# One product with padded weights of 128 columns for the scan inputs of both directions of an orientation

## The chip, the cores and the metric

The kernel runs on one core of one Trainium2 chip. The metric is the device time of one execution in microseconds (us). Everything is float32. The engines of a core are TensorE (PE in the profile, its weight loads PEld), VectorE (DVE), ScalarE (ACT), GpSimd (POOL) and SyncE (SP), which issues the transfers here.

## The reference, cut to what matters

A batch of 8 images of 384 channels and 32 x 32 positions goes through four layers, each with a residual: attention with 12 heads and a depthwise 5 x 5 convolution (layer 0), a selective scan over four directions (layer 1), a blur with fixed shifts (layer 2), attention and a gate (layer 3). The change is in the scan:

```
xs = [x by rows, x by columns, x by rows reversed, x by columns reversed]   # 4 directions, 384 x 1024 each
x_dbl = einsum('bkdl,kcd->bkcl', xs, x_proj_weight)                         # 44 values per position and direction
dts, Bs, Cs = x_dbl[:, :, :12], x_dbl[:, :, 12:28], x_dbl[:, :, 28:]
dt = softplus(einsum('bkrl,kdr->bkdl', dts, dt_projs_weight) + bias)
h = h * exp(dt * A) + (dt * u) * Bs;   y = sum over the 16 states of h * Cs
```

The two directions of one orientation (rows, or columns) read the same positions, one forwards and one backwards; only the 44 columns of weights differ.

## The kernel before

**Stages.** An image's scan has 192 steps: four sets (one for each direction, in the order columns, columns reversed, rows, rows reversed; `DIRS`), each with 3 chunks of 128 channels and 16 states. Set k covers steps 48 k to 48 k + 47. While image i is scanned, the same engines do layer 0 of image i + 1 (`early`, three head groups with four heads each) and layers 2 and 3 of image i - 1 (`late`). The first image's layer 0 runs alone ahead of it, the last image's layers 2 and 3 alone behind it. A loop (`Fori`) covers images 1 to 6; the first and last are written out.

**Order.** Each engine runs one list of events in order of a due time that is counted in scan steps (`scan_events`, `late_events`, `early_events`, sorted by `in_order`). No engine overtakes in its list; semaphores join the lists.

**A scan step**: ScalarE makes the decay (event a, line 1239), VectorE the drive (b, line 1660) and the scan (s, line 1670), GpSimd multiplies the state by its row of C (h, line 1353), and three steps later TensorE adds the transposed state into PSUM banks 4 and 5 (z, line 980). Rows of B and C come from HBM, spread over all partitions, through SyncE (lines 601 and 609).

**Inputs of a set.** Event x, one for each half of 512 positions, is three products of 128 x 44 weights (line 953), which the profile shows as six matmul instructions, into 44 rows of bank 0, and a ScalarE copy to `xdbl` (line 1209), at partitions 0 to 43 for an even set and 64 to 107 for an odd one. The second half waits for the copy of the first. Event W stores the 32 rows of B and C of the set (line 589), K loads the weights for dt (line 593), and d (line 963) multiplies the last 12 rows into dt, through bank 0 again. The x-events of set k are due at 48 k - 21.3 and 48 k - 20.3, those of the next image's set 0 at step 180.7 and 181.7. So set 1 falls beside the blur of the image before, set 2 into the scores of the first head group and set 3 into the middle head group.

**A head group** has a part with scores for the row maxima (S, line 863, read by line 1590) and a part of 32 events T. A T makes transposed scores in banks 0 and 1 (line 883), ScalarE takes their exponentials (line 1180), and the next T waits for that. V (line 892) multiplies by the values into bank 2, Z (line 897) sums into bank 3. After 16 T's the first half of the queries is done: VectorE takes the reciprocal of bank 3 (line 1597) and multiplies it by bank 2 (line 1599). The V that opens the second half waits for line 1599. Between these, VectorE adds terms of the depthwise convolution (line 1609). The same pair of lines closes the second half. This document calls the passage between the two halves the turn.

The lines that say what a T and a V wait for:

```
                    if scans and a:
                        pe.wait_ge(t_exp.h, t_exp.at(img, a))
...
                    if kb == 0 and qh == 1:
                        pe.wait_ge(o_sb.h, o_sb.at(img, 2 * g + 1))
```

**The blur** stores its result to HBM (line 635) and loads it again by channels (line 638); line 1705 adds it. **The start**: line 575 loads the constants, then VectorE prepares small tables and zeroes some tiles (lines 1475 to 1754) and takes the statistics of the first image (line 1502).

Of the kernel before, what the change touches and what calls it, by code (L numbers as in the profile page):

```python
# [6 lines left out]
ACT = mybir.ActivationFunctionType  # L7
# [5 lines left out]
P = 128  # L13
NC = C // P
LB = L // P
HALF = 512
# [8 lines left out]
K, R, N = 4, 12, 16  # L25
XR = R + 2 * N
# [40 lines left out]
def scan_events(first, last):  # L67
# [19 lines left out]
    for run in range(STEPS1 // GN_):  # L87
        u = GN_ * run + GN_ + LAG
# [6 lines left out]
    for k in range(1, K + 1):  # L95
        ahead = -22 if k < K else -12
        if k == K and last:
            continue
        for hf in range(2):
            out.append((PER * k + ahead + hf + 0.70, ("x", k // K, k % K, hf)))  # L100
        out.append((PER * k + ahead + 2.5, ("W", k // K, k % K)))
        out.append((PER * k + ahead + 4.0, ("K", k // K, k % K)))
# [8 lines left out]
    for i in range(STEPS1 + SLOTS):  # L111
        for kind, late in (("B", 1.0), ("C", 2.3)):
            at = i - SLOTS + late
# [186 lines left out]
def build(nc, t):  # L300
    ctx = ExitStack()
    with ctx:
        def sb(name, cols, parts=P):
            return ctx.enter_context(nc.sbuf_tensor(name, [parts, cols], F32))
# [3 lines left out]
        def sem(name, per, first=1):  # L308

            s = Signal(ctx.enter_context(nc.semaphore(name)), per, first)  # L310
            if per:
                signals.append(s)
            return s
# [7 lines left out]
        negA = sb("negA", K * NC * N)  # L321
        w_xproj = sb("w_xproj", NC * K * XR)
        w_dt = sb("w_dt", C)
# [165 lines left out]
        xc_in = sem("x1_loaded", 16 * NC)  # L489
        xd_ps = sem("xproj_in_psum", 2 * K)  # L490
        xd_sb = sem("xproj_evacuated", 2 * K)
        bc_st = sem("bc_rows_stored", 16 * K)
# [75 lines left out]
        def _(sp):  # L568
            for s in signals:
                sp.sem_inc(s.h, s.first)  # L570
            for name, dst in [("ident", ident[:, :]), ("group_avg", group_avg[:, :]), ("vecs", vecs[:, :]),
                              ("vec96", vec96[0:QC3, :]), ("lepe_w", lepe_w[:, :]), ("A_logs", negA[:, :]),
                              ("w_xproj", w_xproj[:, :]),
                              ("row_index", R_[:, 0:1]), ("col_row", R_[:, 32:64])]:
                sp.dma_start(dst, t[name]).then_inc(c_in.h, 16)
# [9 lines left out]
            def scan(img, kind, k, first=False):  # L585
                if kind == "W":
                    at = 64 * (k % 2)
                    sp.wait_ge(xd_sb.h, xd_sb.at(img, 2 * k + 2))
                    sp.dma_start(bc_d[k], xdbl[at:at + 2 * N, :]).then_inc(bc_st.h, 16)
# [147 lines left out]
        def _(pe):  # L737
# [188 lines left out]

            wx = w_xproj[:, :].rearrange("p (c k r) -> p c k r", c=NC, k=K)

            def scan(img, kind, k, u=0, first=False):
# [13 lines left out]
                if kind == "x":  # L943
                    if k == 0 and u == 0:
                        pe.wait_ge(gu_out.h, gu_out.at(img, 1))
                    if u:
                        pe.wait_ge(xd_sb.h, xd_sb.at(img, 2 * k + 1))
                    elif k or not first:
                        pe.wait_ge(dt_abs.h, dt_abs.at(img, 2 * NC * k))
                    for c in range(NC):  # L950
                        rhs = U[:, c, :]
                        rhs = transposed(rhs)[:, u * 16:u * 16 + 16, :] if cols else rhs[:, u * HALF:(u + 1) * HALF]
                        mm = pe.matmul(ps[0:XR, 0, :], wx[:, c, cols + 2 * back, :], rhs, start=c == 0, stop=c == NC - 1)  # L953
                    mm.then_inc(xd_ps.h, 1)
                if kind == "d":
                    c, hf = u // 2, u % 2
                    at = 64 * (k % 2) + 32
                    if u == 0:
                        pe.wait_ge(xd_sb.h, xd_sb.at(img, 2 * k + 2))
                        pe.wait_ge(wd_in.h, wd_in.at(img, 16 * (k + 1)))  # L960
                    else:
                        pe.wait_ge(dt_abs.h, dt_abs.at(img, 2 * NC * k + u))
                    pe.matmul(ps[:, 0, :], w_dt[at:at + R, c * P:(c + 1) * P], xdbl[at:at + R, hf * HALF:(hf + 1) * HALF],  # L963
                              start=True, stop=True).then_inc(dt_ps.h, 1)
# [171 lines left out]
        def _(act):  # L1136
# [60 lines left out]
            def scan(img, kind, k, u=0, first=False):  # L1197
# [4 lines left out]
                if kind == "x":  # L1202
                    act.wait_ge(xd_ps.h, xd_ps.at(img, 2 * k + u + 1))
                    at = 64 * (k % 2)
                    if u == 0 and k >= 2:
                        act.wait_ge(bc_st.h, bc_st.at(img, 16 * (k - 1)))
                    elif u == 0 and not first:
                        act.wait_ge(bc_st.h, bc_st.at(img - 1, 16 * (K + k - 1)))
                    act.activation(xdbl[at:at + XR, u * HALF:(u + 1) * HALF], ps[0:XR, 0, :], ACT.Copy).then_inc(xd_sb.h, 1)
                if kind == "d":  # L1210
# [196 lines left out]
        def _(v):  # L1407
# [163 lines left out]
            def u_free(img):  # L1571

                v.wait_ge(dt_sb.h, dt_sb.at(img, K * NC))
                v.wait_ge(xd_sb.h, xd_sb.at(img, 2 * K))

# [96 lines left out]
            def late(img, kind, u=0, alone=False):  # L1672
# [70 lines left out]
                if kind == "fx":  # L1743
                    m = u
                    if m == 0:
# [3 lines left out]
                                           ALU.mult, ALU.add).then_inc(f_sb.h, 1)  # L1749

            v.memset(negm[:, :], 0.0)
            v.memset(k2[1], 0.0)
# [91 lines left out]
```

## Time and profile before

| | |
|---|---|
| median of 3 runs | 10391.47 us (10388.24 to 10403.53) |
| the profiled execution | 10405.13 us, its span 10403.3 us |
| VectorE busy | 8089.8 us, 78% |
| TensorE busy | 7344.5 us, 71%, mean granted clock 0.786 |
| GpSimd busy | 4789.0 us, 46% |
| ScalarE busy | 4060.0 us, 39% |
| products of line 953 | 384 instructions, 289.2 us busy |

A busy share is a mean over stages with different limits: none of the engines is busy throughout. An image takes some 1,260 us. In the rows, a line of the timeline gives the start, the duration, the engine, the line of the kernel, the operation, what it writes and reads, how many instructions are merged in it, and in brackets how long the engine was idle before it and what ended that. The granted clock is TensorE's as a share of 2.4 GHz, so 0.50 is 1.2 GHz.

### The profile page before, as it was taken

The page shows a single profiled execution, that of the slowest core. Times are in us where ns is not written, and L with a number is a line of the kernel's source. Part 1 is how long each engine was busy: PE and PEld are TensorE (multiplying, and loading weights), DVE is VectorE, ACT ScalarE, POOL GpSimd, SP SyncE. Part 2 cuts the span into 40 slices and gives each one's busy share as a digit, 9 for nine tenths or more (in the row PEclk, how much of TensorE's full clock was granted, in tenths as well). Part 3 has the DMA queues.
Part 4 walks back from the last instruction along what each step waited for, and adds up shares of the span by engine and source line. Part 5 has one row for each costly group of instructions (what it writes and reads, how often), then busy time and mean ns, then how long its engine had stood idle before and what let it go on. Part 6 is the DMA issues. An engine that isn't in the chain of part 4 may idle for free.

```text
span 10403.3 us, 101295 instructions
## 1 busy us (share of the span) xinstructions
PE 7344.5 (71%) x33720; PEld 3729.0 (36%) x33720; DVE 8089.8 (78%) x5527; ACT 4060.0 (39%) x4186; POOL 4789.0 (46%) x1990
## 2 busy tenths in 40 slices
PE   6757775777758777586776777677775777757556
PEld 2233334433334333342234432343333433244333
DVE  5477888778885888768987688876888678887992
ACT  3333443344433444334443345433443334433431
POOL 2154554345553454435644355434555345543660
PEclk8857877888769878688887878787886888868657
DMA  0174457544574445744566445664447544575782
GB/s 26 42 234 160 164 184 235 197 144 165 187 250 164 159 165 201 237 159 160 174 216 220 158 163 170 234 198 162 164 163 246 196 154 160 189 232 198 253 272 58
DMA packets 717961, 1875.97 MB, mean 180 GB/s; under 512 B 258896, under 2 KB 274640, under 8 KB 717264
## 3 DMA queue, kind: packets, MB, share of 16 engines
q1 hardware_dynamic: 717392, 1869.00, 54.0%
q8 instruction: 281, 4.60, 0.2%
q14 instruction: 288, 2.36, 0.1%
HBM read 1772.03 MB, written 71.04 MB: 177 GB/s over the span
## 4 chain that ended last, share of the span: by engine, by line
PE 40%; DVE 32%; issue 14%; ACT 7%; DMA 4%; DVEq 2%; SPq 1%; ACTq 1%; POOL 0%; POOLq 0%
DVE R L1670 14%; PE ps L751 8%; DVE ps L1660 8%; PE ps L883 7%; PE ps L980 5%; ACT R L1180 4%; DVE nmx L1590 4%; PE ps L1068 3%; PE ps L892 3%; PE ps L863 2%; PE ps L953 2%; PE ps L1051 2%; PE ps L963 1%; PE ps L845 1%; PE ps L1037 1%
## 5 line engine op out<-in xcount | busy, mean ns | idle before, releaser
L1353 POOL TENSOR_TENSOR R<-R 128x1024 f32<-128x1024 f32 x1536 | 3673.5, 2392 | 4302.2 <-DVE ps L1660 4198.6
L1670 DVE TENSOR_TENSOR_SCAN R<-R,ps 128x1024 f32<-128x1024 f32 x1536 | 3508.0, 2284 | 176.3 <-ACT R L1239 62.7
L1239 ACT ACTIVATE R<-R,negA 128x1024 f32<-128x1024 f32 x1536 | 1749.4, 1143 | 2313.4 <-DVE R L1670 2273.6
L980 PE MATMUL ps<-ident,R 128*128 128x128 f32 x12288 | 2146.9, 335 | 587.6 <-POOL R L1353 545.9
L980 PEld LDWEIGHTS ps<-ident,R 128*128 128x128 f32 x12288 | 1806.3, 175 | 1576.1 <-issue 775.2
L1660 DVE TENSOR_TENSOR ps<-R 128x1024 f32<-128x1024 f32 x1536 | 2030.5, 1322 | 162.1 <-DMA R<-bc_scratch 53.7
L1180 ACT ACTIVATE R<-ps 128x1024 f32<-128x1024 f32 x768 | 785.6, 1023 | 1061.8 <-PE ps L883 1061.8
L863 PE MATMUL ps<-R 32*128 32x512 f32 x3072 | 660.1, 943 | 678.8 <-DVE nmx L1590 585.7
L883 PE MATMUL ps<-R 64*128 64x512 f32 x3072 | 900.9, 665 | 203.2 <-ACT R L1180 108.0
L1590 DVE TENSOR_REDUCE nmx<-ps 128x4 f32<-128x2048 f32 x384 | 873.4, 2282 | 193.8 <-PE ps L863 190.6
L751 PE MATMUL ps<-R 128*128 128x512 f32 (+1 forms) x1824 | 879.2, 640 | 201.9 <-DVE R L1525 142.2
L1360 POOL TENSOR_TENSOR R<-R 128x1024 f32<-128x1024 f32 x312 | 824.3, 2642 | 331.2 <-ACT R L1173 269.5
L751 PEld LDWEIGHTS ps<-R 128*128 128x128 f32 (+1 forms) x1824 | 356.7, 200 | 664.5 <-issue 600.7
L1609 DVE SCALAR_TENSOR_TENSOR R<-R,lepe_w 128x1024 f32<-128x1024 f32 x264 | 514.7, 1950 | 26.0 <-issue 3.4
L1173 ACT ACTIVATE R<-R,lepe_w 128x1024 f32<-128x1024 f32 x312 | 361.0, 1159 | 346.6 <-POOL R L1360 346.0
L863 PEld LDWEIGHTS ps<-R 32*128 32x128 f32 x3072 | 167.7, 257 | 894.5 <-DVE nmx L1590 742.9
L892 PE MATMUL ps<-R 128*32 128x512 f32 x3072 | 432.0, 636 | 54.5 <-DVE R L1599 51.4
L883 PEld LDWEIGHTS ps<-R 64*128 64x128 f32 x3072 | 240.6, 191 | 636.2 <-ACT R L1180 419.6
L1345 POOL TENSOR_TENSOR R<-R 128x1024 f32<-128x1024 f32 x96 | 253.1, 2637 | 437.4 <-DVE R L1651 437.4
L1597 DVE RECIPROCAL R<-ps 128x512 f32<-128x512 f32 x48 | 161.1, 3357 | 335.1 <-PE ps L897 335.1
L897 PE MATMUL ps<-R,ones 128*32 128x512 f32 x3072 | 411.0, 607 | 0.0
L761 PE MATMUL ps<-ident,R 128*128 128x128 f32 x1280 | 220.6, 331 | 227.4 <-DVE R L1689 68.0
(157 smaller groups left out, 5615.0 us busy)
## 6 DMA issues: line engine op xcount, KB each, us to landing
R<-bc_scratch SPq DMA_DIRECT2D x3072, 512.0 KB, 4.5
R<-in_x SPq DMA_DIRECT2D x72, 512.0 KB, 7.1
out<-R SPq DMA_DIRECT2D x72, 512.0 KB, 5.3
R<-shift_scratch SPq DMA_DIRECT2D x48, 640.0 KB, 7.4
R<-R SPq DMA_DIRECT2D x192, 128.0 KB
R<-out SPq DMA_DIRECT2D x48, 512.0 KB, 8.4
R<-in_w_qkvo SPq DMA_DIRECT2D x32, 576.0 KB, 8.3
rows_scratch<-R SPq DMA_DIRECT2D x24, 512.0 KB, 7.4
```

The lines of the kernel that those rows point to most:

```text
L751: mm = pe.matmul(dst[0:parts, hf * HALF:(hf + 1) * HALF], lhs[:, c], rhs(c, hf), start=c == 0, stop=c == NC - 1)
L863: mm = pe.matmul(ps[:, bank + r, :], q4[HD * r:HD * r + HD, g, qc * P:(qc + 1) * P], k4[HD * r:HD * r + HD, g, hf * HALF:(hf + 1) * HALF], ...
L883: mm = pe.matmul(ps[:, bank + j, :], k2[pair][rows, kb * P:(kb + 1) * P], q2[g][pair][rows, qh * HALF:(qh + 1) * HALF], start=True, stop=True)
L892: pe.matmul(ps[HD * r:HD * r + HD, 2, :], vT[:, kb, P * g + HD * r:P * g + HD * r + HD], pT[(2 * a + r // 2) % 4][:, r % 2, :], start=kb = ...
L980: mm = pe.matmul(ps[:, 4 + b // 4, (b % 4) * P:(b % 4 + 1) * P], state[i % HELD][:, b * P:(b + 1) * P], ident[:, :], start=fresh and i % G ...
L1180: act.activation(pT[a % 4].rearrange("p j q -> p (j q)"), banks(bank), ACT.Exp).then_inc(t_exp.h, 1)
L1239: act.activation(decay[i % len(decay)], dt[:, c, :], ACT.Exp, scale=negA[:, col:col + 1]).then_inc(a_sb.h, 1)
L1353: pool.tensor_tensor(state[i % HELD], state[i % HELD], rows_c[slot], ALU.mult).then_inc(hc_sb.h, 1)
L1360: pool.tensor_tensor(heads[:, m, :], heads[:, m, :], tapped[n % 2], ALU.add).then_inc(dw_sb.h, 1)
L1590: v.tensor_reduce(nmx4[:, :, qc, hf], ps[:, bank:bank + 4, :], AX.X, ALU.max, negate=True)\
L1660: v.tensor_tensor(drive, dtu[:, c, :], rows_b[slot], ALU.mult).then_inc(b_sb.h, 1)
L1670: v.tensor_tensor_scan(h, a, b, 0.0, ALU.mult, ALU.add).then_inc(h_sb.h, 1)
```

## The change

The weights of the two directions of one orientation stand side by side in one tile of 128 columns for each chunk: 44 columns of one, 20 of zeros, 44 of the other, 20 of zeros. One x-event then gives the inputs of two sets: its product fills all 128 partitions of bank 0, and one ScalarE copy brings them to `xdbl`, where the odd set's rows land at partition 64 as before. So x-events are left only for sets 0 and 2; those of sets 1 and 3 are gone, and the events W and d of the odd sets wait for the copy of the even one. The copy for set 2 overwrites all of `xdbl` and so waits for the stores of both sets before it. `w_xproj` is loaded to a free part of the large tile `R` at the start, and VectorE zeroes the padded tile and copies the weights into it, six copies of 2 x 44 columns.

```
-        for hf in range(2):
+        for hf in range(2 * (k % 2 == 0)):
             out.append((PER * k + ahead + hf + 0.70, ("x", k // K, k % K, hf)))
...
-        w_xproj = sb("w_xproj", NC * K * XR)
+        w_xproj = sb("w_xproj", NC * 2 * P)
...
-        xd_ps = sem("xproj_in_psum", 2 * K)
-        xd_sb = sem("xproj_evacuated", 2 * K)
+        xd_ps = sem("xproj_in_psum", K)
+        xd_sb = sem("xproj_evacuated", K)
...
-                              ("w_xproj", w_xproj[:, :]),
+                              ("w_xproj", R_[:, 256:256 + NC * K * XR]),
...
                 if kind == "W":
                     at = 64 * (k % 2)
-                    sp.wait_ge(xd_sb.h, xd_sb.at(img, 2 * k + 2))
+                    sp.wait_ge(xd_sb.h, xd_sb.at(img, k // 2 * 2 + 2))
...
-            wx = w_xproj[:, :].rearrange("p (c k r) -> p c k r", c=NC, k=K)
+            wx = w_xproj[:, :].rearrange("p (c o m) -> p c o m", c=NC, o=2)
...
                     if u:
-                        pe.wait_ge(xd_sb.h, xd_sb.at(img, 2 * k + 1))
+                        pe.wait_ge(xd_sb.h, xd_sb.at(img, k + 1))
...
-                        mm = pe.matmul(ps[0:XR, 0, :], wx[:, c, cols + 2 * back, :], rhs, start=c == 0, stop=c == NC - 1)
+                        mm = pe.matmul(ps[:, 0, :], wx[:, c, cols, :], rhs, start=c == 0, stop=c == NC - 1)
...
                     if u == 0:
-                        pe.wait_ge(xd_sb.h, xd_sb.at(img, 2 * k + 2))
+                        pe.wait_ge(xd_sb.h, xd_sb.at(img, k // 2 * 2 + 2))
...
-                    act.wait_ge(xd_ps.h, xd_ps.at(img, 2 * k + u + 1))
-                    at = 64 * (k % 2)
-                    if u == 0 and k >= 2:
-                        act.wait_ge(bc_st.h, bc_st.at(img, 16 * (k - 1)))
+                    act.wait_ge(xd_ps.h, xd_ps.at(img, k + u + 1))
+                    if u == 0 and k:
+                        act.wait_ge(bc_st.h, bc_st.at(img, 16 * k))
                     elif u == 0 and not first:
-                        act.wait_ge(bc_st.h, bc_st.at(img - 1, 16 * (K + k - 1)))
-                    act.activation(xdbl[at:at + XR, u * HALF:(u + 1) * HALF], ps[0:XR, 0, :], ACT.Copy).then_inc(xd_sb.h, 1)
+                        act.wait_ge(bc_st.h, bc_st.at(img - 1, 16 * K))
+                    act.activation(xdbl[:, u * HALF:(u + 1) * HALF], ps[:, 0, :], ACT.Copy).then_inc(xd_sb.h, 1)
...
+            v.memset(w_xproj[:, :], 0.0)
+            v.drain()
+            raw = R_[:, 256:256 + NC * K * XR].rearrange("p (c b o r) -> p c b o r", c=NC, b=2, o=2)
+            padded = w_xproj[:, :].rearrange("p (c o b r) -> p c o b r", c=NC, o=2, b=2)
+            for c in range(NC):
+                for o in range(2):
+                    v.tensor_copy(padded[:, c, o, :, 0:XR], raw[:, c, :, o, :])
             v.memset(negm[:, :], 0.0)
```

## Rows read from the trace of the kernel before

**Rows 1.** Chain that ended last, 3770 to 3790 us: its shares by line.
```profile
by line: PE ps L883 27.9%; PE ps L953 27.8%; ACT R L1180 20.7%; PE ps L980 10.2%; PE ps L892 9.9%; ACT R L1209 3.0%; issue 1.8%; ACTq L1179 0.2%
```

**Rows 2.** Timeline, middle head group's turn, image 2 (start us, duration us, ...).
```profile
3771.85 1.06 PE L892 MATMUL ps<-R 128*32 128x512 f32 x8
...
3775.83 1.09 PE L980 MATMUL ps<-ident,R 128*128 128x128 f32 x8
...
3777.91 1.06 PE L897 MATMUL ps<-R,ones 128*32 128x512 f32 x8
...
3779.04 3.36 DVE L1597 RECIPROCAL R<-ps 128x512 f32<-128x512 f32 x1 [10.24 <-PE ps L897]
3779.10 2.77 PE L953 MATMUL ps<-R,w_xproj 128*44 128x512 f32 x6
...
3782.55 1.13 PE L883 MATMUL ps<-R 64*128 64x512 f32 x4 [0.68 <-ACT R L1209]
...
3783.61 1.07 PE L892 MATMUL ps<-R 128*32 128x512 f32 x8
...
3784.61 1.09 PE L980 MATMUL ps<-ident,R 128*128 128x128 f32 x8
...
3786.69 1.07 PE L897 MATMUL ps<-R,ones 128*32 128x512 f32 x8
```

**Rows 3.** Timeline, third head group's turn, image 2.
```profile
3992.57 3.36 DVE L1597 RECIPROCAL R<-ps 128x512 f32<-128x512 f32 x1 [7.23 <-PE ps L897]
...
3996.74 1.94 PE L892 MATMUL ps<-R 128*32 128x512 f32 x8 [2.99 <-DVE R L1599]
...
4001.35 1.07 PE L897 MATMUL ps<-R,ones 128*32 128x512 f32 x8
```

**Rows 4.** Timeline, third head group's turn, image 3.
```profile
5250.13 3.36 DVE L1597 RECIPROCAL R<-ps 128x512 f32<-128x512 f32 x1 [7.23 <-PE ps L897]
...
5254.31 1.07 PE L892 MATMUL ps<-R 128*32 128x512 f32 x8 [2.99 <-DVE R L1599]
...
5257.39 1.06 PE L897 MATMUL ps<-R,ones 128*32 128x512 f32 x8
```

**Rows 5.** Timeline, first head group's turn, image 2.
```profile
3559.93 3.36 DVE L1597 RECIPROCAL R<-ps 128x512 f32<-128x512 f32 x1 [5.20 <-PE ps L897]
...
3564.11 1.93 PE L892 MATMUL ps<-R 128*32 128x512 f32 x8 [2.99 <-DVE R L1599]
...
3569.88 1.07 PE L897 MATMUL ps<-R,ones 128*32 128x512 f32 x8
```

**Rows 6.** Windows: us, PE, PEld, DVE, ACT, POOL busy, PEclk, DMA share, GB/s.
```profile
3997.00:4000.00 3.00, 3.00 (x15) 1.39 (x8) 2.91 (x3) 0.00 (x0) 0.00 (x0) 0.50 0.00 0
...
5252.00:5255.00 3.00, 0.69 (x8) 0.16 (x8) 2.83 (x4) 1.50 (x2) 0.00 (x0) 1.00 0.00 0
```

**Rows 7.** Timeline, middle head group's end, image 2.
```profile
3821.89 1.07 PE L897 MATMUL ps<-R,ones 128*32 128x512 f32 x8
...
3823.74 3.35 DVE L1597 RECIPROCAL R<-ps 128x512 f32<-128x512 f32 x1
```

**Rows 8.** Timeline, inputs of set 1 and the blur's end, image 2.
```profile
3070.19 5.36 PE L953 MATMUL ps<-R,w_xproj 128*44 128x512 f32 x6
...
3081.57 3.36 DVE L1705 TENSOR_TENSOR R<-R 128x3072 f32<-128x3072 f32 x1 [4.08 <-DMA R<-blur_scratch]
```

**Rows 9.** Weight loads by line and form: count, busy us, mean ns, idle before.
```profile
L751 PEld LDWEIGHTS ps<-R 128*128 128x128 f32 x1440 | 289.6, 206 | 517.2 <-issue 457.0 <-DVE R L1741 43.2 <-DVE R L1626 10.5
...
L953 PEld LDWEIGHTS ps<-R,w_xproj 128*44 128x44 f32 x384 | 49.3, 143 | 219.6 <-issue 155.2 <-DVE nmx L1590 43.4 <-ACT R L1180 15.0
```

**Rows 10.** Timeline of VectorE at the start.
```profile
23.00 0.91 DVE L1752 MEMSET R<- 128x1024 f32 x1 [0.16 <-issue]
...
26.02 0.17 DVE L1754 MEMSET ones<- 128x128 f32 x1
26.11 3.59 DVE L1502 BATCH_NORM_STATS2 stats<-R 128x6 f32<-128x512 f32 x6
```

More of the change, by code:

```diff
@@ L1573, in u_free @@
                 v.wait_ge(dt_sb.h, dt_sb.at(img, K * NC))
-                v.wait_ge(xd_sb.h, xd_sb.at(img, 2 * K))
+                v.wait_ge(xd_sb.h, xd_sb.at(img, K))
             def early(img, kind, a=0, j=0, scans=1):
```

## The prediction

> **What bounds the kernel now.** I first read the spread of time over lines in the chain that ended last. In the stretch of an attention group in which the inputs of set 3 are computed, the chain runs through TensorE and ScalarE: 27.8% of that stretch is the matmuls of line 953, beside the transposed scores of line 883 at 27.9% and their exponentials [rows 1]. So at this place the x-products aren't free. Then I read the whole stretch in order of time, in the same place of each image. Seven images (0 to 6) run attention of the next image beside the scan, with three head groups each, so there are seven such places. Last I read the other places where x-products are removed (set 1).
>
> In [rows 2] the reader is to see one passage, the turn between the two query halves of the middle head group. TensorE does V, then the first x, the transposes of a scan step, a T and the Z at 3777.91. The end of that Z starts VectorE's reciprocal at 3779.04, for which VectorE had stood idle 10.24 us. The second x follows at 3779.10, and the V of the new half at 3783.61. V of a new half has a wait of its own: for line 1599 on VectorE, because bank 2 is only free then.
>
> **The change at set 3, first x.** The six instructions of one x go, with the ScalarE copy. From V to the transposes takes 3.98 us with the x between (3771.85 to 3775.83) and 1.00 without it (3783.61 to 3784.61) [rows 2]. So the transposes, the T, the Z and the reciprocal come 2.98 us earlier. That part is on the path at both ends: VectorE is idle ahead of the reciprocal, and TensorE was busy.
>
> **Set 3, second x.** From 3779.10 to the next T at 3782.55 it holds TensorE for some 3.45 us, and the chain lists it. But it lies beside the reciprocal, and what is late next is line 1599. I need not guess how the passage looks without it: the first and third head groups of every image have the same turn without an x, 14 in all. There TensorE stands idle 2.99 us ahead of V, until line 1599 is done [rows 3 to 5]. Measured from the reciprocal's start to that of the Z that follows the next T, the turn takes 7.65 us with the x in the middle group [rows 2]; without one it takes 7.26 [rows 4], 8.78 [rows 3] or 9.95 [rows 5]. The second x's removal is therefore worth +0.39, -1.13 or -2.30 us to TensorE, not 3.45. The three values are one mechanism: in the idle gap the granted clock falls from 1.00 to 0.50, that is from 2.4 to 1.2 GHz, or doesn't. Where it fell, V took 1.94 us, and the windows show 0.50 right behind the gap; where it stayed, V took 1.07 and the clock was 1.00 [rows 3, 4, 6]. How long it stays low makes the difference between 8.78 and 9.95. Of the 14 turns 3 are of the first kind, 5 of the second (8.8 to 8.9) and 6 of the third; I take these shares for the seven new ones. The Trainium skill (TensorE: Matmul & The Clock Gate, section "What's actually happening") says that the throttled state is the default and that activity releases it; read alone, it would let every such gap end at half rate. By that all seven would be of the slowest kind and the sum below would be 7.9 us instead of 13.2; the trace agrees with it in 11 of 14.
>
> **What is left of it at the group's end.** Behind the turn VectorE has no idle time in the middle group until the second reciprocal, 44.70 us after the first (3823.74 less 3779.04). TensorE's last Z starts at 3821.89 and is done 1.13 us later by the distance of Z and reciprocal in [rows 2], at 3823.02, so 43.98 us after the first reciprocal [rows 7]. The later of the two sets the time. With the clock kept, TensorE is ready at 43.59 and VectorE binds at 44.70: the gain is the whole 2.98. In the middle kind it is 43.98 + 1.13 = 45.11, gain 2.98 - 0.41 = 2.57. In the slowest it is 43.98 + 2.30 = 46.28, gain 2.98 - 1.58 = 1.40. Mean by the shares: (3 x 2.98 + 5 x 2.57 + 6 x 1.40) / 14 = 2.16 us, seven times 15.1 us. From the second reciprocal everything (turned values, padding copy, scores of the next group) hangs on it, so the shift goes on.
>
> **Set 1.** Here I take nothing, in all eight images. The x-products run at half clock, each 5.36 us, while VectorE waits for rows of B from HBM and for the blur result; it stands idle 4.08 us ahead of line 1705 for that load [rows 8]. SyncE, not TensorE, sets these. The price if this cover were gone is at most both x's, 10.7 us an image. The store of B and C for set 1 (event W) stands far enough behind in SyncE's queue that it isn't reached until both are evacuated; so nothing queued behind it moves. For set 3 the same event held SyncE's queue, behind it the next B row; that row waits for a drive of VectorE in any case. In the last image set 3 runs with no attention or late work beside it, VectorE doing scans back to back: nothing.
>
> **The products that stay.** Sets 0 and 2 now load 128 columns where 44 were loaded: a mean of 206 ns a load against 143 [rows 9], in 192 loads. One x of six instructions takes 2.77 us, 460 ns apiece [rows 2], and the loads run beside that stream, so I take nothing. The bounds are nothing and 192 x 63 ns = 12.1 us. The Trainium skill (TensorE: Matmul & The Clock Gate, section "LDWEIGHTS (loading the stationary operand)") speaks against the change here: it makes the load's time proportional to the columns, P / 1.2 GHz. By an estimate from that page the difference is 70 ns, 13.4 us in all, if nothing hid it. The ScalarE copy has the same 512 elements per partition.
>
> **The start.** VectorE gets one memset of 768 columns, a drain and six copies of 88 elements per partition, ahead of the statistics at 26.11 us that begin with no idle time, so this is on the path. A memset of 1024 columns takes 0.91 and one of 128 takes 0.17 [rows 10]; between them 768 gives 0.70. A copy of 88 elements I take at no more than the 128-column memset, 6 x 0.17 = 1.0, and 0.2 for the drain: 1.9 us. Bounds: 1.2 (copies pipelined) and 2.9 (0.91, and twice the copies).
>
> **The sum.** 15.1 - 1.9 = 13.2 us. The profiled execution took 10405.1 (span 10403.3 and 1.8 around it); it would take 10391.9. It lies 13.7 us above the median of the runs shown, and nothing in the sum depends on that, so I take 10391.5 - 13.2 = **10378.3**. With the clock kept in all seven it is 20.9 - 1.9 = 19.0, thus 10372.5; with the slowest turn in all (a case inside the forecast, chance 0.10) it is 9.8 - 1.9 = 7.9, thus 10383.6.
>
> **Rivals.**
> (A) Both x's count in full, as the chain's lines suggest: 7 x (2.98 + 3.45) = 45.0, less 1.9, time 10348. For it speaks the chain; against it the wait of V and 14 turns that stood idle. Chance 0.10.
> (B) Slower: the wider weight loads aren't hidden. They cost 12.1 us in the products that stay, the start 1.9; against the lowest gain of 9.8 that is 4.2 more than before, 10396. It decides from 41 ns a load on (9.8 - 1.9 = 7.9 us over 192). Against it: a load of 206 ns [rows 9] has 460 ns of stream to hide in; only the first load of each of the 32 runs has none. Chance 0.08.
> (C) The shift of two to three microseconds changes at which of the other gaps the clock falls. If the 14 turns that stay all became of the slowest kind, that would take 3 x 2.69 + 5 x 1.17 = 13.9 us and the time would be 10392, as before; if all kept the clock, it would give 6 x 2.69 + 5 x 1.52 = 23.7, time 10355. Such changes are likely in part and of either sign. Chance that they outweigh the rest: 0.20.
>
> **How the numbers follow.** The forecast has 0.62. A measurement of this kernel tells about 0.2% from no change, 20.8 us: the limits are 10370.7 and 10412.3. Beyond the lower one lie A (0.10), the fast part of C (0.08) and the edge of the forecast (0.07): faster 0.25. Slower by that much only if B and C meet: 0.03. Same: 0.72. Range: from the fast side of C with some of A left out, 10358, to 10397, which takes in B and the slow side of C.
>
> **What the profile will show.** Right, if in the middle group's turn no x is left, the first reciprocal's idle time falls from 10.24 to 7.2 to 7.4 us, V waits some 3 us for line 1599, and the second reciprocal stands 44.7 to 46.3 us behind the first. x-products halve to 192 instructions, each as long as before. At set 1, line 1705 still waits for the blur load. The statistics begin some 1.9 us later. It is wrong if V of the new half doesn't wait, if a six-instruction x takes longer than 2.8 us at full clock, or if line 1705 comes earlier relative to the blur stores.

## The result, and the profile after

The changed kernel takes 10347.18 us (median of 5 runs, 10343.73 to 10356.55) against 10403.53 for the kernel before beside it (5 runs, 10388.24 to 10415.91): ratio 0.9949 [0.9936, 0.9962], some 53 us faster by the ratio (the two medians stand 56 us apart). The prediction was 10378.3 with 10358 as the lower end of its range, and "same" as the likeliest outcome. The profiled execution took 10356.55, its span 10354.7, so 48.6 less than before.

The page's first part (busy time of each engine):

```profile
PE 7261.8 (70%) x33528; PEld 3752.7 (36%) x33528; DVE 8073.3 (78%) x5534; ACT 4041.1 (39%) x4154; POOL 4802.7 (46%) x1990
```

TensorE is busy for 83 us less. Its x-products alone fell by 128 (289.2 to 161.6, below); its other products got longer, at a mean granted clock of 0.778 in place of 0.786. Now the middle head group's turn of image 2, as in [rows 2], on VectorE and TensorE:

```profile
3772.48 3.36 DVE L1596 RECIPROCAL R<-ps 128x512 f32<-128x512 f32 x1 [7.27 <-PE ps L897]
3772.54 1.13 PE L883 MATMUL ps<-R 64*128 64x512 f32 x4
...
3776.66 1.31 PE L892 MATMUL ps<-R 128*32 128x512 f32 x8 [2.99 <-DVE R L1598]
...
3781.32 1.07 PE L897 MATMUL ps<-R,ones 128*32 128x512 f32 x8
...
3817.65 3.36 DVE L1596 RECIPROCAL R<-ps 128x512 f32<-128x512 f32 x1 [0.38 <-PE ps L897]
```

The reader is to see that no x is left, that the reciprocal's idle time fell from 10.24 to 7.27, that V waits 2.99 us for the second line behind the reciprocal (1598 here), as in [rows 3 to 5], and that the second reciprocal comes 45.17 us behind the first. All this is as forecast. It does not add up to 53 us.

To find where the time went I took the start times of the 1,536 scans (line 1670 before, 1669 after) from the timelines and compared them bin by bin. One bin stands out: from scan 18 to scan 33 of an image, beside which the blur of the image before runs. Summed over images 1 to 7 it takes 716.4 us before and 676.1 after. By the start of the last scan the changed kernel is 41.4 us ahead; another 7.2 come behind it, where the last image's own blur stands alone. The x of set 1 lies in that bin, and I had taken nothing for it. But the transfers of the blur changed too. The page's last part (transfers: how many, KB each, median us from issue to landing), first before:

```profile
rows_scratch<-R SPq DMA_DIRECT2D x24, 512.0 KB, 7.4
R<-rows_scratch SPq DMA_DIRECT2D x32, 384.0 KB, 8.1
blur_scratch<-R SPq DMA_DIRECT2D x32, 384.0 KB, 6.9
```

and after:

```profile
rows_scratch<-R SPq DMA_DIRECT2D x24, 512.0 KB, 7.4
R<-rows_scratch SPq DMA_DIRECT2D x32, 384.0 KB, 5.9
blur_scratch<-R SPq DMA_DIRECT2D x32, 384.0 KB, 5.7
```

The same bytes land 2.2 and 1.2 us sooner in two of three. The change touches none of these transfers. How it reaches VectorE can be read from SyncE's queue and VectorE. Before, image 2:

```profile
3014.06 0.43 SPq L632 DMA_DIRECT2D R<-rows_scratch  x1
3014.60 4.63 SPq L601 DMA_DIRECT2D R<-bc_scratch  x1
...
3019.74 4.66 SPq L609 DMA_DIRECT2D R<-bc_scratch  x1
3024.28 1.23 DVE L1660 TENSOR_TENSOR ps<-R 128x1024 f32<-128x1024 f32 x1 [4.05 <-DMA R<-bc_scratch]
```

and after:

```profile
3013.61 0.43 SPq L632 DMA_DIRECT2D R<-rows_scratch  x1
3014.15 3.59 SPq L601 DMA_DIRECT2D R<-bc_scratch  x1
...
3018.26 3.54 SPq L609 DMA_DIRECT2D R<-bc_scratch  x1
3021.64 1.23 DVE L1659 TENSOR_TENSOR ps<-R 128x1024 f32<-128x1024 f32 x1 [1.95 <-DMA R<-bc_scratch]
```

The row loads behind a blur transfer hold the queue for 3.6 us in place of 4.6, and the drive waits 1.95 in place of 4.05. The end of the blur, as in [rows 8]:

```profile
3076.66 3.36 DVE L1704 TENSOR_TENSOR R<-R 128x3072 f32<-128x3072 f32 x1 [5.08 <-DMA R<-blur_scratch]
```

It still waits for the load, only earlier.

What the change did do to these transfers is their place. `w_xproj` grew from 528 to 768 columns, 960 bytes a partition. The tiles are allocated one behind the other, so that `R`, in which nearly everything lies, starts at byte 22656 in place of 21696. 22656 is a multiple of 128 and 21696 isn't (it leaves 64). The two transfers that got faster move pieces of 32 values, 128 bytes; the one that didn't (`rows_scratch<-R`) moves whole rows of 4 KB. The records of single packets in the same two traces say so too: the 196,736 packets of 128 bytes took a mean of 18.0 ns before and 13.5 after, the 431,104 of 4096 bytes 191.2 and 189.7.

The answering rows of the weights [rows 9]:

```profile
L953 PE MATMUL ps<-R,w_xproj 128*128 128x512 f32 x192 | 161.6, 998 | 39.7 <-DVE nmx L1589 35.5 <-DVE R L1524 3.5 <-ACT R L1208 0.7
L953 PEld LDWEIGHTS ps<-R,w_xproj 128*128 128x128 f32 x192 | 45.3, 251 | 120.4 <-issue 70.2 <-DVE nmx L1589 43.6 <-DVE R L1524 3.6
```

and of the start [rows 10]:

```profile
23.29 0.70 DVE L1750 MEMSET w_xproj<- 128x768 f32 x1 [0.27 <-issue]
24.07 0.78 DVE L1756 COPY w_xproj<-R 128x88 f32<-128x88 f32 x6
...
28.25 3.59 DVE L1501 BATCH_NORM_STATS2 stats<-R 128x6 f32<-128x512 f32 x6
```

The statistics start 2.14 us later (forecast 1.9).

### The profile page after: what moved, and what is told of

Its sections match the earlier page's. It is cut to its first block, busy times and chain, and to the rows that moved or that the text cites. A ratio compares the mean times of both kernels' runs of the same rounds, so it can differ in the third digit from the quotient of the medians.

```text
span 10354.7 us, 100800 instructions
## 1 busy us (share of the span) xinstructions
PE 7261.8 (70%) x33528; PEld 3752.7 (36%) x33528; DVE 8073.3 (78%) x5534; ACT 4041.1 (39%) x4154; POOL 4802.7 (46%) x1990
## 4 chain that ended last, share of the span: by engine, by line
PE 41%; DVE 32%; issue 14%; ACT 7%; DMA 3%; DVEq 2%; SPq 1%; POOL 1%; ACTq 1%; POOLq 0%
DVE R L1669 14%; PE ps L751 8%; PE ps L883 7%; DVE ps L1659 7%; PE ps L980 5%; ACT R L1180 4%; DVE nmx L1589 4%; PE ps L892 3%; PE ps L1068 3%; PE ps L863 2%; PE ps L1051 2%; DVE R L1596 1%; PE ps L953 1%; PE ps L963 1%; PE ps L845 1%
## 5 line engine op out<-in xcount | busy, mean ns | idle before, releaser
L980 PE MATMUL ps<-ident,R 128*128 128x128 f32 x12288 | 2170.1, 338 | 644.8 <-POOL R L1352 603.8
L761 PE MATMUL ps<-ident,R 128*128 128x128 f32 x1280 | 224.7, 335 | 229.5 <-DVE R L1688 70.5
```

The source lines that it names most:

```text
L980: mm = pe.matmul(ps[:, 4 + b // 4, (b % 4) * P:(b % 4 + 1) * P], state[i % HELD][:, b * P:(b + 1) * P], ident[:, :], start=fresh and i % G ...
```

## The experiments

All ratios are to the kernel before on the same chip. Besides the time, two sums over images read from each profiled execution serve below: the blur bin (scan 18 to 33, images 1 to 7), and the first head group's first half (from its first exponential to its first reciprocal, images 1 to 6).

### The place of R alone, and the change at four places

```
move_only       (before)   w_xproj = sb("w_xproj", NC * K * XR)
                         + sb("spare", NC * 2 * P - NC * K * XR)
change_unmoved  (changed)+ sb("spare", 16)
change_at_0     (changed)+ sb("spare", 32)
change_at_64    (changed)+ sb("spare", 48)
```

> The kernel before with 240 unused columns (960 bytes) behind the tile of the weights, so that every tile allocated after it, R too, lies where it lies in the changed kernel: R starts at byte 22656 instead of 21696, 128 instead of 64 bytes past a multiple of 128... that is at 0 instead of 64 modulo 128. No product, copy or wait is changed. Theory P (place): the time goes where the transfers of 128-byte pieces are, the blur's. Then R<-rows_scratch lands in about 5.9 us instead of 8.1 and blur_scratch<-R in about 5.7 instead of 6.9, the seven stretches from scan 18 to scan 33 of an image sum to about 676 us instead of 716, and the time is 40 to 50 us below before. Theory X (products): the gain comes from the x-products of set 1 that are gone; then this kernel is as before, both medians stay at 8.1 and 6.9, and the stretches sum to 716.

> The changed kernel with 16 unused columns (64 bytes) behind the padded weights: R starts at byte 22720, which is 64 modulo 128 and 192 modulo 256 as before. Theory P: the two transfers are back at 8.1 and 6.9 us, the seven blur stretches sum to about 716 us, and what is left is the set-3 turn (7 x 2 to 3 us) less the start: 8 to 19 us below before. Theory X: it keeps the whole 50 us and the stretches stay near 676.

> The changed kernel with 32 unused columns: R starts at byte 22784, a multiple of 256. Theory P in the form that a 128-byte piece costs more when it crosses a multiple of 256 bytes: as the changed kernel (no piece crosses at 0 or 128), 5.9 and 5.7 us, 676 us; larger rows that now start on a multiple of 256 might win a little more, 0 to 10 us. If instead the start at 128 modulo 256 was what mattered, it is slower than the changed kernel.

> The changed kernel with 48 unused columns: R starts at byte 22848, 64 modulo 256. Theory P in the form above: every second 128-byte piece crosses a multiple of 256, as at 192, so like the change unmoved: 8.1 and 6.9 us and 716 us in the blur stretches. If only the distance of 192 were bad, it is like the changed kernel.

| kernel | R starts at byte | left over of 128 | us | ratio | blur bin, us |
|---|---|---|---|---|---|
| before (beside changed; 10407.7 beside the other four) | 21696 | 64 | 10403.5 | 1 | 716.4 |
| move_only | 22656 | 0 | 10349.4 | 0.9942 [0.9928, 0.9957] | 674.5 |
| changed | 22656 | 0 | 10347.2 | 0.9949 [0.9936, 0.9962] | 676.1 |
| change_at_0 | 22784 | 0 | 10350.7 | 0.9940 [0.9924, 0.9956] | 671.3 |
| change_unmoved | 22720 | 64 | 10411.1 | 1.0001 [0.9991, 1.0011] | 716.4 |
| change_at_64 | 22848 | 64 | 10416.3 | 1.0006 [0.9997, 1.0014] | 713.3 |

The whole gain is the place. 240 columns that nothing uses give it without any of the change, and the change at the old remainder gives nothing, where its expectation had 8 to 19 us. What changes is the blur's transfers: the packets of 128 bytes took a mean of 13.4 ns in move_only and change_at_0 and 18.0 in change_unmoved and change_at_64. Of the 60.7 us that move_only's profiled span is shorter, 42 lie in the blur bin and 6.7 behind the last scan, where the last image's blur is; the other 12 are spread over the rest of the images and not traced. One line's view of move_only (line 633 there), who waited for it, and its landing:

```profile
  PE ps L1006: 139.8, 8
  PEld ps L1006: 35.5, 2
DMA to landing us min/median/max: 3.4/5.9/6.8
```

and of change_at_64, the same transfer:

```profile
  PE ps L1006: 171.7, 8
  PEld ps L1006: 44.4, 2
DMA to landing us min/median/max: 4.9/8.0/9.0
```

Places 0 and 128 above a multiple of 256 are alike, and so are 64 and 192: with R 64 bytes off, every second piece of 128 bytes crosses a multiple of 256, with R on a multiple of 128 none does. With R 64 bytes off every piece also crosses a multiple of 128, so these places don't tell at which boundary the time goes. The Trainium skill (DMA: Bandwidth & Descriptors, section "How a descriptor splits into AXI transactions") states that an AXI transaction, into which a transfer's descriptors are split, has to begin at an address aligned to 256 bytes and that bytes fetched ahead of the wanted ones still cost; by that a piece across a boundary needs two. The four places agree with it, also for the load, whose end in SBUF is written and not read; the page has no time for it, the runs give 2.1 us of 8.0 on 384 KB.

### The removed products, at the old place

```
+DROPPED = [(3, 0)]   # drop_set3_first;  _second [(3, 1)]; _both the two; drop_set1 [(1, 0), (1, 1)]; drop_four all
...
-        for hf in range(2):
+        for hf in [h for h in range(2) if (k, h) not in DROPPED]:
+            v.memset(xdbl, 0.0)      # drop_set1 and drop_four, once at the start
```

Each leaves the products, copies and inputs of the named x's out (those sets read what `xdbl` holds), with narrow weights; the counts that others wait for go down with them.

> The kernel before, at its old place, without the two x-products and copies of set 1 in any image (the rows of set 1 stay zero or old, and a memset of 1024 columns, 0.9 us, is added at the start). My theory for set 1: they are hidden beside the blur's transfers, so the stretch from scan 18 to scan 33 stays at 102 us an image (716 for seven) and the time is that of before within 5 us, but for changes of the clock pattern. Rival: they were on the path there; then that stretch is shorter by up to 10.7 us an image and the time by up to 75 us.

> The kernel before, at its old place, without the first x of set 3 (half of that set's inputs is left as set 1 wrote it). The prediction's step: the first reciprocal of the middle head group comes 2.98 us earlier in seven images, its distance to the second reciprocal stays 44.7 us, so the gain is 7 x 2.98 = 20.9 us at the turn, and the second x still fills the wait of V. If gains at the turn are given back at the clock elsewhere in the image (my rival C, as the changed kernel at the old place now suggests), the turn shows the 2.98 and the median is nonetheless within 10 us of before, with the first head group's part (scan 82 to 92) longer by 2 to 4 us an image.

> The kernel before, at its old place, without the second x of set 3. The prediction's step: it lies beside the reciprocal. The first reciprocal keeps its place, V starts 4.2 us after it instead of 4.57, TensorE idles 3 us before V and its clock may fall, and the distance of the reciprocals is 44.7, 45.1 or 46.3 us instead of 44.7: no gain, up to 11 us of loss. Rival A (both products count in full): 3.45 us an image earlier, 24 us in all.

> The kernel before, tiles at their old place, without both x of set 3 (left out: those products, their copies and their outward transfers; set 3 uses the x of set 1). The prediction's own theory (what it takes off lies at the middle head group's turn alone, nothing is given back): 15 us off, 0.9985. From the run without the first x (10393.05, 0.9982) and the one without the second (0.9998): 0.9982, 10391 us, with the first reciprocal of the turn 2.98 us earlier. Rival, that a shorter turn is given back in the first head group's scans (scans 82 to 92, six images: 452.7 us before, 465.1 in the changed kernel): 0.9995 to 1.000, with those scans at 460 or more.

> The kernel before, tiles at their old place, narrow weights, without the x of sets 1 and 3 (left out: those four products, their copies and outward transfers; one memset of xdbl at the start, 0.9 us, in their place). It has the change's removed work and none of its wide weights, six copies at the start or early weights. If the wide weights are what swallowed the gain of the change at its old place (1.0001): this run is near the sum of the single runs, 0.9991 and 0.9982, so 0.997 (10380 us). If the removal itself is given back elsewhere in the image (the first head group's scans): 0.999 to 1.000, with scans 82 to 92 above 455 us for six images, as in the changed kernel.

| kernel | us | ratio | blur bin | first head group's first half |
|---|---|---|---|---|
| before (beside drop_set1 and the singles 10409.4) | 10407.5 | 1 | 716.4 | 371.1 |
| drop_set1 | 10402.4 | 0.9991 [0.9982, 0.9999] | 706.2 | 361.2 |
| drop_set3_first | 10393.1 | 0.9982 [0.9972, 0.9992] | 714.9 | 373.9 |
| drop_set3_second | 10412.5 | 0.9998 [0.9989, 1.0007] | 714.9 | 368.4 |
| drop_set3_both | 10380.9 | 0.9976 [0.9967, 0.9985] | 717.2 | 366.5 |
| drop_four | 10383.2 | 0.9979 [0.9970, 0.9988] | 719.5 | 365.0 |

Set 3's first x is worth some 19 us (0.0018 of 10409, by its interval 8 to 29; the prediction had 7 x 2.98 = 20.9 at the turn), its second nothing alone, both 25 (16 to 34). Set 1's are worth 9 alone, at the edge of what these runs tell, and nothing beside set 3's. The stretch from scan 122 to scan 124, in which the middle group's turn lies, is 18.4 us shorter than before in drop_set3_first, summed over the images, and 0.1 us longer in drop_set3_second. So the removal is real, 22 to 25 us, and yet the change at the old place is at 1.0001. Something in it takes them back.

### What takes them back: wide weights, start, or both

```
wide_all         (before) padded weights, all x kept:  wx[:, c, cols, :] -> ps[:, 0, :], copy of ps[at:at + XR], start as changed, spare 16
wide_drop_four   wide_all with the four x's of drop_four left out
start_drop_four  drop_four, narrow weights, with the change's load to R, memset of 768 columns and six copies
change_108       (changed) wx[:, c, cols, 0:64 + XR] -> ps[0:64 + XR, 0, :], copy of as many partitions
```

> The kernel before with the padded weights of 128 columns and the copies at the start, R at 64 modulo 128 as before, but with all sixteen half products per two images kept, eight an image, and ScalarE copying only its 44 rows. It isolates the wide weights. Start: +2.1 us, as the changed kernel's statistics show. Wide loads hidden: nothing more, time within 5 us of before plus 2. Wide loads exposed (rival B): 384 loads x 63 ns = 24 us more. If it is the wide products that make the first head group's part (scan 82 to 92) longer in all four profiles of the changed kernel (461 to 470 us for six images, 442 and 453 without the change), that sum is 460 or more here too, else it is about 450.

> The kernel before, R at its old remainder (64 of 128), without the x of sets 1 and 3 (left out, as in drop_four), but with the padded weights: 128 columns in the products that stay and the memset and copies at the start. If the wide weights and the start swallow the gain of drop_four (0.9979): 1.000 (10405 us), with scans 82 to 92 near 460 us for six images and the granted clock below 1.00 there. If they are hidden as predicted, 0.998 (10385 us), and the double copy is what costs.

> As drop_four (products of sets 1 and 3 left out, narrow weights, R at its old remainder), with the change's work at the start alone: weights loaded to R, one memset of 768 columns, six copies. If the start costs only its 2 us: 0.998 (10385 us). If the later start moves the places where the clock falls: up to 1.000.

> The changed kernel (R on a multiple of 128 bytes) with products and copy of 108 columns and partitions in place of 128; the 20 columns of zeros left out. If the loads' columns cost time: the mean load falls from 251 to about 230 ns and the time by some 3 us, 10344; if they are hidden: 10347, 0.995.

| kernel | us | ratio | first head group's first half |
|---|---|---|---|
| drop_four (narrow) | 10383.2 | 0.9979 [0.9970, 0.9988] | 365.0 |
| start_drop_four (narrow) | 10392.6 | 0.9984 [0.9975, 0.9993] | 369.2 |
| wide_drop_four | 10395.2 | 0.9989 [0.9980, 0.9998] | 382.8 |
| wide_all | 10412.6 | 1.0004 [0.9995, 1.0012] | 377.3 |
| change_unmoved (wide) | 10411.1 | 1.0001 [0.9991, 1.0011] | 377.4 |
| change_108 (wide, 108) | 10350.9 | 0.9945 [0.9932, 0.9959] | 375.3 |

The times alone separate little here: each step is half a thousandth to a thousandth, the intervals are as wide. With the same start, wide weights took the time from 0.9984 to 0.9989 (wide_drop_four, whose expectation had 0.998 or 1.000 and got neither), and with no x left out from 1 to 1.0004 with the start in it. change_unmoved at 1.0001 and change_at_64 at 1.0006 lie 12 to 18 us above wide_drop_four by the ratios. What they have and it hasn't is the one copy of 128 partitions for two sets and the waits around it: as much as half of what is taken back can lie there, and no run tests that copy by itself. The bin separates wide from narrow. Over all 18 profiled kernels of this study, ten with narrow weights have 361.2 to 374.4 us in the first head group's first half (mean 367.3) and eight with wide ones 375.3 to 385.0 (mean 380.9), wherever R lies and whatever else they leave out. A single half takes 59.2 us in 28 of the 60 narrow cases and in none of the 48 wide ones, where, but for one of 59.8, it takes 62.3 to 65.9. That is 13.6 us in six images. It is a loss in that bin, not shown to be one in the time: the bin is 17.8 us longer in wide_drop_four than in drop_four, and the two profiled spans are 0.7 us apart (10390.6 and 10391.3).

The wide products themselves stand ahead of this stretch. What differs inside it is the clock. I show the two ends of the spread, in different images. First drop_four, image 1, a half of 59.21 us: the timeline's row of the product that opens it,

```profile
2236.63 1.13 PE L890 MATMUL ps<-R 64*128 64x512 f32 x4 [1.43 <-DMA R<-nrow]
```

and the windows around it (columns as in [rows 6]):

```profile
2228.00:2238.00 10.00, 5.26 (x24) 4.10 (x25) 9.67 (x8) 1.34 (x2) 6.38 (x3) 0.64 0.42 144
2238.00:2248.00 10.00, 7.74 (x50) 3.24 (x49) 6.58 (x5) 6.89 (x7) 5.42 (x3) 1.00 0.87 311
2248.00:2252.00 4.00, 2.63 (x21) 1.47 (x23) 2.30 (x2) 0.00 (x0) 0.00 (x0) 1.00 0.47 183
2252.00:2258.00 6.00, 5.87 (x35) 2.20 (x34) 5.64 (x5) 3.08 (x3) 0.75 (x1) 1.00 0.00 0
```

Then wide_drop_four, image 2, a half of 65.88 us, the same two views:

```profile
3494.99 2.08 PE L891 MATMUL ps<-R 64*128 64x512 f32 x4 [1.44 <-DMA R<-nrow]
```

```profile
3487.30:3497.30 10.00, 6.20 (x23) 4.30 (x24) 9.60 (x8) 1.34 (x2) 6.94 (x3) 0.50 0.52 163
3497.30:3507.30 10.00, 8.05 (x44) 3.46 (x42) 5.81 (x4) 6.73 (x7) 4.70 (x2) 0.91 0.85 313
3507.30:3511.30 4.00, 2.40 (x14) 2.17 (x15) 1.28 (x1) 0.17 (x1) 0.00 (x0) 0.77 0.32 127
3511.30:3517.30 6.00, 6.00 (x19) 1.84 (x18) 5.06 (x4) 2.06 (x2) 0.00 (x0) 0.59 0.00 0
```

The same four instructions take 1.13 us at 2.4 GHz and 2.08 at 1.2. In the narrow half of 59.2 the clock is back before it begins and stays; in this wide one it comes back later and falls again. The length of a half goes with its mean granted clock in all 108: 1.00 in the 28 of 59.2, 0.94 or 0.95 in those of 62.3 to 62.5 (drop_four's image 2 is one, 62.46), 0.88 in those near 65.9. Narrow weights don't guarantee the short half, 32 of 60 lack it; wide ones never had it. Why the wide products ahead shift this, the runs don't show; that the bin is longer shows in all eight. The start adds 4.2 us to that bin in one profile and 9 us to the median (0.9979 to 0.9984), less than the intervals: left open. change_108 was no faster than the changed kernel, though its mean load fell from 251 to 223 ns.

### Is the idle gap what brings the clock down?

```
                     if kb == 0 and qh == 1:
+                        if scans:            # move_filled: if scans and g != 1
+                            pe.wait_ge(t_exp.h, t_exp.at(img, 2 * a + 3))
+                            for i in range(2):
+                                pe.matmul(ps[:, 0, :], ident[:, :], group_avg[:, 0:HALF], start=True, stop=True)
                         pe.wait_ge(o_sb.h, o_sb.at(img, 2 * g + 1))
```

Two products that nobody reads, into bank 0, before V's wait: on the kernel before, on the changed one, and on move_only (there not in the middle head group).

> The kernel before with two further 128x128 by 512 products (results unused) ahead of the V chain in each turn, after its wait for the exponential, so that TensorE's idle stretch ahead of V falls from about 3 us to about 1.2. If the idle stretch is what brings the granted clock from 1.00 to 0.50: V takes 1.07 us in every turn, the first transpose ends 7.26 us after the reciprocal's start, and the two reciprocals stand 45.2 to 45.4 us apart in place of 46.3 to 46.9: up to 1.2 us for each of 14 turns, 0.9984 to 0.9995. If the clock falls for another reason: V stays at 1.9 us in most turns and the time is the same or up to 8 us more (1.000 to 1.001).

> The changed kernel (R on a multiple of 128 bytes, 10347 us, 0.9949) with the same two unused products ahead of V in each turn. If the idle stretch sets the clock: V at 1.07 us in the four middle turns in which it fell, and 5 to 20 us off the changed kernel: 0.993 to 0.9945. If not: 0.995 to 0.996.

> The kernel before with the 240 unused columns that move R to a multiple of 128 bytes, and the two unused products ahead of V in the turns of the first and third head group alone (14 turns), not in the middle one, where they held V back 3.2 us in before_filled. If the clock's fall in these turns costs what the distance of the reciprocals says (46.28 against 44.69 and 46.88 against 45.48): 1.5 us for each of 11 turns, 16 us below move_only: 10333, 0.9927. If it is given back elsewhere: 10345 to 10349, 0.994.

| kernel | us | ratio | turns with V over 1.1 us | between reciprocals, groups 1 / 2 / 3 (us, six images) |
|---|---|---|---|---|
| before | 10407.5 | 1 | 11 | 275.6 / 268.2 / 276.7 |
| before_filled | 10405.8 | 0.9998 [0.9989, 1.0007] | 0 | 268.1 / 283.0 / 272.9 |
| changed | 10347.2 | 0.9949 [0.9936, 0.9962] | 14 | 272.1 / 270.2 / 275.1 |
| change_filled | 10342.9 | 0.9939 [0.9925, 0.9952] | 0 | 268.1 / 268.1 / 272.9 |
| move_only | 10349.4 | 0.9942 [0.9928, 0.9957] | 7 | 273.8 / 268.2 / 272.1 |
| move_filled | 10332.6 | 0.9919 [0.9905, 0.9932] | 0 | 268.2 / 268.2 / 272.8 |

The third head group's turn of before_filled, image 2, against [rows 3]:

```profile
3993.70 1.98 PE L893 MATMUL ps<-group_avg,ident 128*128 128x512 f32 x4 [1.20 <-ACT R L1185]
3995.62 1.07 PE L897 MATMUL ps<-R 128*32 128x512 f32 x8
...
3998.70 1.06 PE L902 MATMUL ps<-R,ones 128*32 128x512 f32 x8
```

The idle gap is 1.20 us in place of 2.99, and V takes 1.07. So it is in all 56 filled turns of the three kernels (gaps of 1.12 to 1.20). So the clock falls here for the unfilled gap; the runs don't separate the shorter gap from the work put into it. The gap of 2.99 isn't enough by itself: the changed kernel has it in all 21 turns and kept the clock in 7. before_filled gained 16.6 us in the outer groups' turns by their two reciprocals (275.6 + 276.7 less 268.1 + 272.9 is 11.3 in six images, and 5.3 in image 0), and lost 17.9 in the middle ones, where the extra wait held V back; that is its 0.9998. In the middle group:

```profile
3780.65 1.13 PE L884 MATMUL ps<-R 64*128 64x512 f32 x4 [0.68 <-ACT R L1214]
3782.98 1.98 PE L893 MATMUL ps<-group_avg,ident 128*128 128x512 f32 x4 [1.20 <-ACT R L1185]
3784.89 1.06 PE L897 MATMUL ps<-R 128*32 128x512 f32 x8
```

With the x still there the gap is filled twice, and V comes 3.2 us later behind the reciprocal than in [rows 2] (7.75 against 4.57). Left out there, move_filled takes 10332.6, the lowest median of this study, 17 us under move_only, where its expectation had 16. The two intervals just touch (0.9905 to 0.9932 and 0.9928 to 0.9957), so the gain is likely, its size loose. The two profiled spans differ by 11.9 us, and the two reciprocals of the outer groups' turns stand closer by 10.1 of them (4.9 in six images, 5.2 in image 0); move_only had seven slow V's in its own profile where the expectation counted eleven, so part of the agreement on 16 is luck. change_filled's 0.9939 against 0.9949 lies within the intervals and shows no gain for sure. move_filled has nothing of the change in it but the 960 bytes.

## Why the prediction was wrong

**The term that was missing: the place of R.** The part by part costing took the wider tile as a start cost and as longer loads. The step that failed is that it stopped there and had no term for the tiles allocated behind `w_xproj`, which move by 960 bytes. Alone that measured 0.9942, 58 us. Rival A's 10348 was met within a microsecond by luck: its mechanism, both x's in full, was refuted by drop_set3_second.

**"So I take nothing" for the wide weights: wrong, by a way that wasn't in it.** The load took a mean of 251 ns against 143 (forecast 206) and was all but hidden behind its own stream, as argued: the six instructions of an x at 1.2 GHz take 5.3 to 5.5 us with either, and at full clock, where wide_all still has those of set 3, 2.84 against 2.77. That is just over the 2.8 that the prediction named as a sign of being wrong, and 1 us in all. But the wide kernels have 13.6 us more in the first head group's first half, by the clock. Rival B had the sign with the wrong mechanism; rival C had the mechanism (the clock pattern moves elsewhere) and called it even in sign. In that bin it isn't: all eight wide kernels are longer.

**First x of set 3: right.** The first reciprocal comes 4.02 us behind the 17th exponential in place of 6.99, 2.97 earlier (forecast 2.98), and leaving it out alone gave 19 us.

**Second x of set 3: right.** V waits 2.99 us as in the other head groups; without that x alone nothing was gained.

**The clock in the seven new turns: nearly right.** It was kept in three (V 1.06 or 1.07) and fell in four. The reciprocals stand 43.58 us apart in image 0 and 44.69 to 45.22 in the others; forecast were 44.70, 45.11 or 46.28, and the slowest kind never came. From first exponential to second reciprocal the middle groups are 10.2 - 2.0 = 8.2 us shorter in six images and 3.4 in the first (59.17 + 43.98 less 56.22 + 43.58), 11.6 against a forecast of 15.1: part of it is given back within the group's first half, again at half clock.

**Set 1, "I take nothing": right within what can be told.** Alone 9 us, beside set 3's removal none. Line 1705 starts 4.91 us earlier in image 2, but the blur's stores came earlier too: it starts 19.04 us behind the issue of the last of them before and 20.32 after.

**The start: right**, 2.14 against 1.9, in part by luck: VectorE's rows ahead of the memset are already 0.48 us later (22.86 against 22.38), so its own part is 1.66. The 0.2 us for the drain came from no row; the gap between the memset and the copies is 0.08.

**The sum at the old place.** 13.2 us off was forecast. The removed products alone gave 22 off (drop_four), with the start 17 (start_drop_four, 0.9984), with wide weights too 11 (wide_drop_four), and the change itself 1 us on, each with an interval of some 10 either way. The last step is the largest and has no cause shown. The change by itself is worth nothing that can be told here, at the old place or at the new one (10347.2 against move_only's 10349.4). "Same" would have been the right call for its mechanism; the time was that of 960 bytes.

## What to carry to other kernels

When a change resizes a tile, work out where every tile allocated behind it starts, and run the old kernel with as many unused columns beside the new one: without that run this change would pass for a gain of 0.5%. Keep tiles with transfers in pieces of 128 bytes on a multiple of 128. And where TensorE waits some 3 us for another engine in a stretch that is bound by it, a product that nobody reads is worth a trial (here some 17 us, with intervals that just touch), as long as it waits for nothing later than the wait it stands before.

## What the runs showed of the hardware

The landing of 384 KB in pieces of 128 bytes took 5.9 us (HBM to SBUF) and 5.7 (SBUF to HBM) with the SBUF side on a multiple of 128 bytes, 8.1 and 6.9 with it 64 bytes off, and loads of other data issued beside them held SyncE's queue for 3.6 or 4.6 us. A packet of 128 bytes took a mean of 13.4 or 13.5 ns against 18.0, one of 4096 bytes 190 to 191 at either place.

A gap of 2.99 us took the granted clock down in 11 of 14 turns of the kernel before; one of 1.20, with 1.98 us of products behind it, in none of 56. The Trainium skill (TensorE: Matmul & The Clock Gate, section "What's actually happening") has activity release a throttle that is the default; the filled kernels agree.
